# First layer of a two-layer transformer: where the second token tile's norm, transposition and rank product stand at the seams between stages

## The reference

```
x1 = layernorm(x + attention(x))      # 32 query heads of 16, 8 key/value heads, rotary, causal softmax
inter = x1 @ c1.T @ c2.T              # rank 16, then 1792 columns in 56 blocks of 32
idx   = argmax of each block          # one row of w1 and w2t per block
h     = relu(w1[idx] . x1)
x2 = layernorm(x1 + h @ w2t[idx])
```

## Time and profile before

| | |
|---|---|
| median of three runs | 2222.38 us |
| profiled execution, its own time | 2221.68 us |
| its span, first to last instruction | 2219.8 us |
| mean granted TensorE clock | 0.979 |
| TensorE matmul busy | 2105.7 us, 95% of the span |
| VectorE busy | 1578.0 us, 71% |
| ScalarE busy | 1190.4 us, 54% |
| GpSimd busy | 826.0 us, 37% |
| first layer, up to the first instruction behind the barrier | 524.58 us |

### The profile page before, as it was taken

The page is one execution under the profiler, slowest core; times in us unless marked ns, Lnnn a source line. Parts: engine busy times, 40 slices in busy tenths (PEclk is TensorE's granted clock), DMA queues, the critical chain, the costliest instruction groups (busy, mean ns, idle before and its releaser), DMA issues. The chain is left out here.

```text
span 2219.8 us, 38190 instructions
## 1 busy us (share of the span) xinstructions
PE 2105.7 (95%) x11176; PEld 1587.2 (72%) x11176; DVE 1578.0 (71%) x3197; ACT 1190.4 (54%) x2856; POOL 826.0 (37%) x698
## 2 busy tenths in 40 slices
PE   6899998998999999999999999999999999989998
PEld 4555555545777777877777787787787777767877
DVE  3566666565888599489589768948958967867345
ACT  3554545412676477377457546737736845653330
POOL 4452533311344145245325424514533542453230
PEclk9799999999999999999999999999999999999999
DMA  6000000002889587787867958769777795722101
GB/s 253 9 3 1 16 1 1 1 0 63 232 215 226 115 231 192 112 228 191 162 169 197 181 121 218 185 108 241 187 134 198 197 177 149 177 70 82 51 10 39
DMA packets 241908, 285.39 MB, mean 129 GB/s; under 512 B 9376, under 2 KB 210336, under 8 KB 241056
## 3 DMA queue, kind: packets, MB, share of 16 engines
q1 hardware_dynamic: 241696, 282.86, 52.2%
HBM read 280.20 MB, written 103.02 MB: 173 GB/s over the span
## 5 line engine op out<-in xcount | busy, mean ns | idle before, releaser
L1869 PE MATMUL b_ps<-xh_keep,wh 128*128 128x512 f32 x1152 | 459.1, 399 | 4.0 <-DVE yt L1615 2.1
L1871 PE MATMUL b_ps<-xh_keep,wl 128*128 128x512 f32 x1152 | 450.0, 391 | 0.0
L1870 PE MATMUL b_ps<-xl_keep,wh 128*128 128x512 f32 x1152 | 449.0, 390 | 0.0
L1454 POOL TENSOR_TENSOR wl<-raw_weights,wh 128x512 fp32r<-128x512 f32 x144 | 187.3, 1301 | 350.4 <-ACT wh L1215 348.7
L1568 DVE SCALAR_TENSOR_TENSOR xs<-b_ps,par,xs 128x510 f32<-128x510 f32 (+2 forms) x384 | 284.8, 742 | 44.6 <-ACT xs L1236 31.2
L1596 DVE TENSOR_TENSOR decayed<-b_ps,b_scores 128x384 f32<-128x384 f32 x512 | 266.8, 549 | 35.5 <-ACT b_ps L1265 20.2
L1264 ACT ACTIVATE b_ps<-rows,ncs 128x256 f32<-128x256 f32 x512 | 238.9, 467 | 85.5 <-DMA rows<-skewed_rows 51.5
L1869 PEld LDWEIGHTS b_ps<-xh_keep,wh 128*128 128x128 f32 x1152 | 217.1, 188 | 50.8 <-issue 3.9
L1871 PEld LDWEIGHTS b_ps<-xh_keep,wl 128*128 128x128 f32 x1152 | 216.5, 188 | 46.7
L1870 PEld LDWEIGHTS b_ps<-xl_keep,wh 128*128 128x128 f32 x1152 | 217.2, 189 | 42.8
L1475 POOL TENSOR_TENSOR ssq<-ssq,sq 128x512 f32<-128x512 f32 x112 | 144.4, 1289 | 211.3 <-ACT sq L1273 211.3
(11 more groups left out here) (259 smaller groups left out, 4095.1 us busy)
## 6 DMA issues: line engine op xcount, KB each, us to landing
rows<-skewed_rows SPq DMA_DIRECT2D x252, 384.0 KB, 4.1
skewed_rows<-sum_rows SPq DMA_DIRECT2D x63, 1024.0 KB, 11.6
raw_weights<-win_dram SPq DMA_DIRECT2D x144, 256.0 KB, 7.2
skewed_rows<-sum_rows SPq DMA_DIRECT2D x63, 512.0 KB, 13.4
qkv_or_out_weights<-wout_dram SPq DMA_DIRECT2D x8, 2048.0 KB, 16.0
w<-w_dram SPq DMA_DIRECT2D x2, 3584.0 KB, 23.1
raw_weights<-wgu_dram SPq DMA_DIRECT2D x11, 512.0 KB, 3.5
draw<-wd_dram SPq DMA_DIRECT2D x1, 2816.0 KB, 10.6
```

What stands on the lines that cost most here:

```text
L1454: nc.gpsimd.tensor_tensor(wl[:, n % RING, :], wraw[:, n % RING, :], wh[:, n % RING, :].bitcast(F32), ALU.subtract).then_inc(w_lo.sem, 1)
L1869: nc.tensor.matmul(out, w_h, x_h, start=(k == 0), stop=False)
L1870: nc.tensor.matmul(out, w_h, x_l, start=False, stop=False)
L1871: last = nc.tensor.matmul(out, w_l, x_h, start=False, stop=(k == KT - 1))
```

## The change

The second tile's share of the seam is taken apart. `rank` is split into `turn_x1` (transposition of x1) and `rank` (the product). In the seam TensorE now turns x1's tile 0, turns q and k of the next sequence's second tile, and then makes the rank product of tile 0. The choice of quarter 0 moves behind the first scores of the next stage (and into banks t1, t0 instead of h0, h1, except in the last stage); the transposition of x2's second tile behind the first inner product of slot 0; the transposition of x1's tile 1 to the end of slot 1, its rank product into slot 2. ScalarE's copies and VectorE's steps follow: the norm of tile 1 is cut after its first Newton step, and the rest is done in slot 0 behind `blocks`. Norm steps are the same instructions as before, now from one helper `normalised` for both norms. Only stage 3 still turns x2's last tile at its end.

```diff
@@ TensorE
+            def turn_x1(a, t):
+
                 pe.wait_ge(*x1_ready.made((a, t)))
                 transposes((a, "x1T", t), "t1", [x1[:, t, k * P:(k + 1) * P] for k in range(KT)])
+
+            def rank(a, t):
+
+                cols = slice(t * P, (t + 1) * P)
                 pe.wait_ge(*bk.drained((a, "x1T", t)))
                 product((a, "z", t), "v", P, [(c1[:, k, :], x1T[:, k, cols]) for k in range(KT)])
...
-                outs = [begin((b, "in", q, a), f"s{a}" if b == BATCH - 1 else f"h{a}") for a in range(2)]
+                outs = [begin((b, "in", q, a), f"s{a}" if b == BATCH - 1 else f"h{a}" if q else f"t{1 - a}") for a in range(2)]
...
+                    if ffn is not None and d == 0:
+                        choose(b, 0)
+                    if ffn is not None and d == 2:
+                        rank(b, 1)
                     if ffn is not None and q < 4:
                         if i < 2:
                             inner(b, q, i)
+                        if b and d == 0:
+                            back(b - 1, 1)
+                        if d == 1:
+                            turn_x1(b, 1)
...
-                    rank(att, 0)
-                    choose(att, 0)
+                    turn_x1(att, 0)
                 if nxt is not None:
                     turn(nxt, 1)
                 if att is not None:
-                    rank(att, 1)
-                if ffn is not None:
+                    rank(att, 0)
+                if b == BATCH - 1:
                     back(b, 1)
@@ ScalarE, behind the exponentials of a slot and before its divisions
+                    if ffn is not None and d == 0 and b:
+                        keep_high(b - 1, 1)
+                    if ffn is not None and d == 1:
+                        turned_x1(b, 1)
+                    if ffn is not None and d == 2:
+                        ranked(b, 1)
@@ VectorE, behind the minima of a slot
+                    if ffn is not None and d == 0:
+                        blocks(b, 0)
+                        for _ in attend_1:
+                            pass
+                        if b:
+                            keep_low(b - 1, 1)
+                    if ffn is not None and d == 1:
+                        first(b, 0)
...
-                    if ffn is not None and i == 0 and q < 4:
+                    if ffn is not None and i == 0 and 0 < q < 4:
                         first(b, q)
...
-                    attended(att, 0)
-                    attended(att, 1)
+                    for _ in attended(att, 0):
+                        pass
                 if ffn is not None and b < BATCH - 1:
                     keep_low(b, 0)
                 if att is not None:
-                    blocks(att, 0)
-                if ffn is not None:
+                    attend_1 = attended(att, 1)
+                    next(attend_1)
+                    next(attend_1)
+                if b == BATCH - 1:
                     keep_low(b, 1)
```

More of the change, by code:

```diff
@@ L415, in weigh @@
                     last.then_inc(*bk.full(name))
+            def turn_x1(a, t):
+                pe.wait_ge(*x1_ready.made((a, t)))
+                transposes((a, "x1T", t), "t1", [x1[:, t, k * P:(k + 1) * P] for k in range(KT)])
             def rank(a, t):
                 cols = slice(t * P, (t + 1) * P)
-                pe.wait_ge(*x1_ready.made((a, t)))
-                transposes((a, "x1T", t), "t1", [x1[:, t, k * P:(k + 1) * P] for k in range(KT)])
                 pe.wait_ge(*bk.drained((a, "x1T", t)))
@@ L625, in turned, with turned_x1 @@
                 evacuate((a, "kT", t), kT[:].rearrange("p s u c -> p (s u) c")[:, :, t * P:(t + 1) * P])
+            def turned_x1(a, t):
+                evacuate((a, "x1T", t), x1T[:, :, t * P:(t + 1) * P])
             def ranked(a, t):
                 cols = slice(t * P, (t + 1) * P)
-                evacuate((a, "x1T", t), x1T[:, :, cols])
                 act.wait_ge(*bk.filled((a, "z", t)))
@@ L660, in _ @@
                         back_d = d - lag(att)
+                    if ffn is not None and d == 0 and b:
[4 more added lines that the diff above has]
+                        ranked(b, 1)
+                    if att is not None:
                         if att and 0 <= back_d < PAIRS_OF:
@@ L690, in _ @@
                 if att is not None:
-                    ranked(att, 0)
+                    turned_x1(att, 0)
                 if nxt is not None:
@@ L694, in _ @@
                 if att is not None:
-                    ranked(att, 1)
-                if ffn is not None:
+                    ranked(att, 0)
+                if b == BATCH - 1:
                     keep_high(b, 1)
@@ L788, in attended, with normalised @@
                     bk.free(name)[0], bk.drained(name))
[L789 to L799, removed]
+                yield from normalised(res, x1[:, t, :], t, st[:, t, :], x1_ready, (a, t))
+            def normalised(src, dst, t, st_t, ready, name):
+                step(nc.vector.bn_stats(st_t[:, 0:6], src[:, t, :]))
                 dve.sem_inc(passed)
@@ L811, in fed @@
                         yield
-                own(nc.vector.tensor_scalar(dst, ry[:, t, :], st_t[:, 6:7], rs, ALU.subtract, ALU.mult),
-                    x2_ready.sem, x2_ready.made((b, t)))
+                own(nc.vector.tensor_scalar(dst, src[:, t, :], st_t[:, 6:7], rs, ALU.subtract, ALU.mult),
+                    ready.sem, ready.made(name))
                 yield
+            def fed(b, t):
+                name = (b, "y", t)
+                n = b * TPB + t
+                dst, st_t = keep["x"][:, n, :], st[:, TPB + t, :]
+                dve.wait_ge(*bk.filled(name))
+                own(nc.vector.tensor_tensor(ry[:, t, :], bk.out(name), x1[:, t, :], ALU.add), bk.free(name)[0], bk.drained(name))
+                yield from normalised(ry, dst, t, st_t, x2_ready, (b, t))
             def keep_low(b, t):
```

## The result

The changed kernel took 2212.49 us (median of 6 runs, 2210.5 to 2215.47) against 2222.45 us for the kernel before on the same chip (6 runs, 2221.47 to 2227.55): a ratio of 0.995, with 0.9936 to 0.9964 as its 95% interval. Forecast were 2211.8 us and a range from 2206.5 to 2217.5.

A forecast was written before the change was run, and what follows sets the result against it. TensorE bounds the stages, so time is won only where it stands still or runs at its lower clock. Seams 0 to 3 give 2.4 + 3.8 + 1.9 + 2.5 = 10.6 us, forecasting 2211.8 us, range 2206.5 to 2217.5.

The forecast's parts named there:

- Seam 0 (2.4): Between stages 0's predecessor and its first scores: scores 4.87 us earlier, less 2.48 of moved work, gains 2.4 us.
- seam 1 (3.8): Seam ahead of stage 1: scores 6.7 us earlier, less 2.93 moved, gains 3.8 us, about half from the 1.2 GHz stretch.
- the new one for kT: At the first scores: a new wait for ScalarE's copies of qT and kT, 0.3 us in seam 1.
- Seam 2 (1.9): Seam ahead of stage 2: VectorE sets the term, the choice comes at 356.8 instead of 358.73, gaining 1.9 us.
- the one on the rule: VectorE and GpSimd's shared SBUF port lock: claimed not to hold tiny operands, as one took 0.16 us beside GpSimd's divisions.
- Seam 3 (2.5): Seam ahead of stage 3: two waits of together 1.2 us go, the 1.2 GHz stretch may; 2.5 us, between 1.2 and 3.8.
- VectorE then has its second mask ready about 1 us before TensorE is there: Seam 3: VectorE's second mask should be ready about 1 us before TensorE arrives at 464.7.
- The rival with the hold: Slot 0: GpSimd's weighting holds the rest of VectorE's norm; 4 us less gain, 2215.8 us, chance 0.10.
- The second layer only shifts: Second layer: starts behind a point where all engines meet, so it was claimed only to shift.
- What was to show it: New trace: first scores within 0.4 us of the rank product's end; stage 2's choice in slot 2 waits 1 to 2.
- A clock under 1.00 in stage 0: Sign against the forecast: the granted clock in stages 0 and 1 leaves 1.00.
- The wait over 1 us: Sign against the forecast: TensorE waits over 1 us at the first turned probabilities or x1's transposition in slot 1.

The follow-up runs named there:

- e3: The changed kernel, but the second tile's norm, transposition and rank product stay in the seam; 2230.34 us against 2234.31 for the kernel before on that chip.
- the two repeats: The kernel before, unchanged, profiled two more times; stages 2 and 3 together took 191.80 and 191.81 us.
- e8: The changed kernel, but GpSimd's weighting multiplies by a constant, one tensor input instead of two; 2219.5 us against 2234.31 for the kernel before on that chip.
- e10: The changed kernel with GpSimd's weighting left out; 2205.24 us against 2224.07 for the kernel before on that chip.
- e4: The changed kernel again, no edit; 2217.41 us, ratio 0.9969 to the kernel before.
- e12: The changed kernel a third time, no edit; 2213.03 us, ratio 0.9953 to the kernel before.
- e9: The changed kernel with half of stage 2's second choice in free bank y and the weighting released just before the norm's last step; 2212.05 us, ratio 0.994.
- e1: The changed kernel, but GpSimd's weighting starts only behind the rest of the norm; 2213.16 us, ratio 0.995 to the kernel before.

## Why the prediction was right, and where it was right by luck

- **Seam 0 (2.4) and seam 1 (3.8)**: right in size, and in cause but for the clock. Measured at the second choices 2.3 us (30.53 - 28.24) and 3.7 (32.92 - 29.19), at the next output product 3.76 for stage 1 in all three pairs. The waits that go are the ones named, the new one for kT is 0.47 us, and seam 1's transpositions are back at 2.4 GHz. By e3 the stretch is some 1.5 of the 3.7, where the forecast had about half of 3.8. That it goes with the gaps is not shown: in e3 gaps of 1.91 and 0.69 us were back in seam 1, and the clock stayed up.
- **Seam 2 (1.9)**: 0.4 us in the first pair of profiles (28.63 - 28.23); against the two repeats it is 1.9, but 1.5 of that is their stretch in seam 2. The reciprocal came at +21.14 (347.10), where the forecast had +19.2 (349.3 less the 330.10 of the output product before); the hold is 1.78 of these 1.94 us, so VectorE's other prices were right. The step that failed is the one on the rule: "The trace speaks against it for these tiny operands". The operations of the earlier trace rows are tiny on VectorE's side, but the one on GpSimd's side was another form (tensor by a scalar per partition, 128x256), and e8 shows that this side matters. The row was also one of the free ones: at 202.71 the trace of the kernel before has the same operation at 0.33. Against the weighting, two tensors of 128x896, a tiny operation waits 1.8 us. The Trainium skill, "SBUF — State Buffer", section "SBUF: two separate sides", foretold it: the first to start takes the shared pair and the other stands still for that whole instruction. The changed kernel agrees (1.94 us against 0.16); e8's 0.78 beside an operation of 2.48, and the earlier trace rows, do not. Why the hold is shorter there is not shown.
- **Seam 3 (2.5)**: 2.63 us in the first pair (25.53 - 22.90), and the reason is wrong. "VectorE then has its second mask ready about 1 us before TensorE is there" failed: TensorE waits 1.43 us for it. The 2.6 are the stretch at 1.2 GHz of the first profile; against the two others, where it is not there, the changed kernel loses 0.24 us (22.66 - 22.90). Without the weighting the two waits give 1.35 (22.66 - 21.31), close to the forecast's 1.2.
- **What balanced it.** The rival with the hold was priced at 4 us, and e10 puts it at 3.5 (less than priced in stages 0 to 2, more in stage 3; and the weighting took 2.12 us, where the rate of the divisions that it names gives 3.2). Its time was nonetheless not the outcome, because the kernel before paid some 3 us for stretches at 1.2 GHz in stages 2 and 3 each time, of which the forecast's seam 3 had counted about half, and 1.7 us more for a late one in stage 2 (23.4 us from the third to the fourth transposition of hidden rows in all three profiles), which the changed kernel shows there once in three. Stages 2 and 3 together went from 191.6 to 191.8 us before to 188.3, 186.9 (e4) and 188.8, 2.8 to 4.9 less, where 1.9 + 2.5 = 4.4 were forecast. The stretches that come and go cost the changed kernel up to 3.2 us over the 409.6 of e4 (in the first profile 1.7 late in stage 0 and 1.4 in stage 2 from slot 2 on, in e12 1.7 late in stage 2). So the mean of three profiles is a gain of 9.45 us for the first layer, against 10.6. That the sum came out so near is luck: a hold that was taken for free is made up by stretches that were not in the sum.
- **"The second layer only shifts"**: not within 2 us. The first layer ended 7.49 us earlier (521.74 - 514.25), the span 9.7. What moves the second layer was not tried, and it varies by more than that from one execution of the same kernel to another (1698.1 to 1710.3 us).
- **What was to show it**: no wait over 0.5 us from x1's transposition to the first choice, 1.04 instead of 1.97, and 1.35 us at the choice of stage 2 were as forecast (in e4 and e12 that wait is 2.41, above the 1 to 2); the first scores missed their 0.4 us by 0.07 in seam 1. A clock under 1.00 in stage 0 should have made it wrong; it came and went with nothing changed, so that sign was a bad one. The wait over 1 us came at a place that was not named, the scores of slot 2 in stage 2.

Left open: why the stretch at 1.2 GHz falls into seam 1 of the kernel before each time, into seam 2 twice and seam 3 once, and late in a stage in some executions and not in others. It repeats in one more place: in stage 2 the first seven transpositions of hidden rows, behind a wait of 1.8 to 2.3 us for ScalarE's copy, take 1.73 us instead of 0.98 in all three profiles of both kernels.

## What to carry to other kernels

Before work of VectorE is moved beside work of GpSimd, compare the form of both operations with those that the trace shows side by side; a pair that ran freely says nothing about another pair. Where one profile shows a stretch at the lower clock, take it again before putting it into a sum: here it moved from one seam to another while the sum of two stages stayed. And a forecast that hits its total may still have two wrong terms, which only distances between fixed points, stage by stage, bring to light.

## What the runs showed of the hardware

- VectorE's 128x1 operation took 1.93 or 1.94 us instead of 0.16 beside GpSimd's 128x896 product of two tensors, and a 128x512 one 2.35 instead of 0.55 (e9). Free beside it were the one that reads PSUM and SBUF, 0.69 us, and the reciprocal with one small input, 0.17 (both e1). Beside GpSimd's forms with one tensor a 128x1 operation was held for 0.6 us of 2.48 and a 128x512 one for 0.4 (e8); beside the 128x256 divisions it was 0.17 us (202.71, before) or nothing.
- The same instructions with the same waits ran at either clock: the second rank product behind 0.69 us took 2.08 us in one execution and 1.16 in the next two. Stages 2 and 3 of the kernel before took 191.64 to 191.81 us together in three executions, though the stretches at 1.2 GHz stood in other places.
